# Loads moved at two places of an attention and feed-forward kernel: its first rows of x, and o at the seam before the last stage

## The reference

```
h   = layernorm(x)
q, k, v = h@Wq.T + bq + ocr_bias, h@Wk.T + bk, h@Wv.T + bv
s   = q k / sqrt(32) + 0.1 where |i - j| <= 2          (per head)
x   = x + softmax(s) v @ Wo.T + bo
h2  = quantise(layernorm(x))      # blocks of 32, FP6 grid, scale from the block's largest |value|
x   = x + h2 @ quantise(W).T + bias
```

## Time and profile before

| | us |
|---|---|
| median of three runs | 4157.7 |
| the profiled execution | 4158.59 |
| its span, first to last instruction | 4156.7 |
| granted TensorE clock, mean | 0.990 |
| TensorE (PE) busy | 4040.4 (97%) |
| VectorE (DVE) busy | 3359.5 (81%) |
| GpSimd (POOL) busy | 3034.7 (73%) |
| ScalarE (ACT) busy | 2407.3 (58%) |

### The profile page before, as it was taken

One profiled execution on the slowest core, in us unless ns is written; L12 is line 12 of the kernel. 1 busy time (PEld: TensorE's weight loads), 2 busy tenths in 40 slices (PEclk: granted clock), 3 DMA queues, 4 the chain that ended last, 5 costly groups with the idle time before them and its releaser, 6 DMA issues.

```text
span 4156.7 us, 59570 instructions
## 1 busy us (share of the span) xinstructions
PE 4040.4 (97%) x21328; PEld 2538.1 (61%) x21328; DVE 3359.5 (81%) x5630; ACT 2407.3 (58%) x4651; POOL 3034.7 (73%) x1121
## 2 busy tenths in 40 slices
PE   8999999999999999999999999999999999988999
PEld 6788875555555555555555555555555555546877
DVE  6444568888888888888888888888888898867887
ACT  2222216667667666767676666766676766662322
POOL 2111107888988889899888888888888888874553
PEclk9999999999999999999999999999999999988999
DMA  7888759899999999999999999999999899986665
GB/s 244 266 265 256 230 158 178 182 213 189 200 197 198 197 193 206 189 212 185 206 186 208 189 200 199 193 201 190 203 189 207 182 210 183 213 190 176 176 170 110
DMA packets 292318, 825.16 MB, mean 199 GB/s; under 512 B 28880, under 2 KB 95440, under 8 KB 229584
## 3 DMA queue, kind: packets, MB, share of 16 engines
q0 software_dynamic: 73008, 486.57, 59.5%
q1 hardware_dynamic: 219040, 335.09, 28.7%
HBM read 211.82 MB, written 156.24 MB: 89 GB/s over the span
## 4 chain that ended last, share of the span: by engine, by line
PE 78%; DVE 14%; ACT 3%; DMA 3%; POOL 1%; issue 1%; SPq 1%; POOLq 0%; ACTq 0%; DVEq 0%
PE ps_a L871 20%; PE ps_a L857 20%; PE ps_b L836 17%; PE ps_p L481 12%; DVE part_max L1048 8%; PE ps_b L902 4%; PE ps_b L949 3%; DVE p_sb L1075 3%; ACT p_sb L1024 2%; PE ps_b L882 1%; DMA q_st<-shift 1%; POOL pair L1221 1%; PE ps_a L932 1%; DMA p_sb<-o_d 1%; DMA q_lo_d<-s_lo 0%
## 5 line engine op out<-in xcount | busy, mean ns | idle before, releaser
L1048 DVE TENSOR_REDUCE part_max<-ps_b 128x1 f32<-128x512 f32 x4016 | 2464.1, 678 | 379.9 <-PE ps_b L836 379.7
L1024 ACT ACTIVATE p_sb<-ps_a 128x512 f32<-128x512 f32 x4096 | 2083.6, 614 | 731.5 <-PE ps_a L857 727.4
L1221 POOL TENSOR_TENSOR pair<-p_sb 128x2048 f32<-128x2048 f32 x512 | 2452.5, 4810 | 73.4 <-ACT p_sb L1024 57.9
L871 PE MATMUL ps_a<-p_sb,v_sb 128*32 128x512 f32 x8192 | 996.8, 603 | 37.8 <-DVE p_sb L1075 23.6
L857 PE MATMUL ps_a<-q_st,k_odd 97*128 97x512 f32 x2048 | 844.3, 415 | 12.4 <-DMA q_st<-shift 9.4
L857 PE MATMUL ps_a<-q_st,k_even 97*128 97x512 f32 x2048 | 845.4, 413 | 6.7 <-PEq L163 3.8
L836 PE MATMUL ps_b<-k_odd,q_st 96*128 96x512 f32 x2048 | 813.1, 397 | 0.0
L836 PE MATMUL ps_b<-k_even,q_st 96*128 96x512 f32 x1968 | 783.3, 398 | 0.0
L857 PEld LDWEIGHTS ps_a<-q_st,k_odd 97*128 97x128 f32 x2048 | 387.9, 190 | 337.2 <-issue 213.4
L857 PEld LDWEIGHTS ps_a<-q_st,k_even 97*128 97x128 f32 x2048 | 388.3, 190 | 322.7 <-issue 219.3
L871 PEld LDWEIGHTS ps_a<-p_sb,v_sb 128*32 128x32 f32 x8192 | 224.0, 109 | 524.2 <-ACT p_sb L1024 318.9
(11 more groups left out here) (114 smaller groups left out, 2861.4 us busy)
## 6 DMA issues: line engine op xcount, KB each, us to landing
pair<-pair POOLq DMA_DIRECT2D x448, 1024.0 KB, 8.8
q_st<-q_hi_d SPq DMA_DIRECT2D x128, 256.0 KB, 7.1
xin<-in_x SPq DMA_DIRECT2D x16, 1024.0 KB, 8.6
xb_d<-xb SPq DMA_DIRECT2D x16, 1024.0 KB, 5.7
q_hi_d<-s_hi SPq DMA_DIRECT2D x64, 256.0 KB, 6.3
q_lo_d<-s_lo SPq DMA_DIRECT2D x64, 256.0 KB, 7.3
k_hi_d<-s_hi SPq DMA_DIRECT2D x64, 256.0 KB, 3.4
k_lo_d<-s_lo SPq DMA_DIRECT2D x64, 256.0 KB, 4.3
```

The source lines that it names most:

```text
L871: last = nc.tensor.matmul(ps_a[h * HD:(h + 1) * HD, RING_S, :], v_sb[:, kt, h * HD:(h + 1) * HD], p_sb[:, s % SLOTS, h, :], start=(kt == 0 ...
L1024: nc.scalar.activation(p_sb[:, s % SLOTS, h, :], ps_s[:, (HG * s + h) % RING_S, :], ACT.Exp, scale=SCALE).then_inc(p_ready, 1)
L1048: nc.vector.tensor_reduce(part_max[:, unit % 2, col, n:n + 1], ps_m[:, max_place(unit, j) % RING_M, :], AX.X, ALU.max).then_inc(max_taken, 1)
L1221: nc.gpsimd.tensor_tensor(pair[:, m % PAIR_RING], p_sb[:, s % SLOTS], p_sb[:, (s + 1) % SLOTS], ALU.add).then_inc(paired, 1)
```

## The change

At the start, the load of chunk 0's x becomes four loads of one tile each, each with its own semaphore, and `moments(0)` waits for them one by one; the common counter `x_loaded` counts from chunk 1 on. ScalarE takes a square root of a constant before the first real one. At the seam between attention and finish: `load_o(1)` stands after `put_shift` of the last unit instead of five steps ahead of it; the four loads of `load_rec(2)` stand at steps 11 to 14 of the last unit instead of after `load_xb(1)`; `load_o(2)` stands ahead of `load_xb(1)`. For that, odd chunks from 3 on use `p_sb[:, 3]` and even ones `o_first`, where it was the other way round. TensorE projects three tiles of chunk 1 instead of two ahead of `turn_x(0)`. ScalarE does `normalise(1)` ahead of `o_highs(2)` instead of after it.

```diff
+            for t in range(TT):
+                sp.dma_start(xin[:, t, :], x_ch[0][:, t, :]).then_inc(x_first[t], 16)
-            sp.dma_start(xin[:], x_ch[0]).then_inc(x_loaded, 16)
...
             def moments(c):
-                v.wait_ge(x_loaded, 16 * c + 16)
+                if not isinstance(c, int) or c > 0:
+                    v.wait_ge(x_loaded, 16 * c)
                 for t in range(TT):
+                    if isinstance(c, int) and c == 0:
+                        v.wait_ge(x_first[t], 16)
...
             act.wait_ge(consts, 6)
+            nc.scalar.activation(root[:], eps[:], ACT.Sqrt)
             std_of(0)
...
         def o_raw(c):
-            return p_sb[:, 3] if c > 1 and c % 2 == 0 else o_first
+            return p_sb[:, 3] if c > 1 and c % 2 == 1 else o_first
...
-                    at_least(sp, o_split, NHG * (c - 1))
+                    at_least(sp, o_split, NHG * (2 if c == 2 else c - 1))
...
-                    if unit == NU - 2 and kt == 10:
+                    if unit == NU - 2 and kt == KT - 1:
                         load_o(1)
+                    if unit == NU - 1 and 11 <= kt < 11 + NHG:
+                        load_rec(2, (kt - 11,))
...
+            load_o(2)
             load_xb(1)
-            load_rec(2)
             sp.wait_ge(pv_done, ST)
             sp.wait_ge(paired, NM)
-            load_o(2)
             load_xb(2)
...
-                    out_project(c + 1, (0, 1))
+                    out_project(c + 1, (0, 1, 2) if c == 0 else (0, 1))
...
-                    out_project(c + 1, (2, 3))
+                    out_project(c + 1, (3,) if c == 0 else (2, 3))
...
                 high(c)
+                if c == 0:
+                    normalise(1)
                 if c + 2 < NCH:
                     o_highs(c + 2)
-                if c + 1 < NCH:
+                if 1 < c + 1 < NCH:
                     normalise(c + 1)
```

More of the change, by code:

```diff
@@ L136, in project @@
     w_loaded = [sem(f"w_loaded{i}") for i in range(3)]
+    x_first = [sem(f"x_first{i}") for i in range(TT)]
     consts, bias_ready = sem("consts"), sem("bias_ready")
@@ L173, in project @@
         std, rstd, eps = sb("std", [P, TT]), sb("rstd", [P, TT]), sb("eps", [P, 1])
+        root = sb("root", [P, 1])
         x_hi, x_lo = sb("x_hi", [P, KB, CH], F32R), sb("x_lo", [P, KB, CH], F32R)
@@ L202, in add_bias @@
             def add_bias(c):
-                pool.wait_ge(x_loaded, 16 * c + 16)
+                at_least(pool, x_loaded, 16 * c)
                 at_least(pool, xb_out, 16 * c)
```

## The result

The change makes the kernel slower: 4161.17 us median (4146.72 to 4172.83, 20 runs) against 4152.58 (4142.87 to 4166.67, 20 runs), ratio 1.002 (1.0011 to 1.0029), 4.6 to 12 us. 4143.5 was forecast, with 4159 as the range's upper end. The forecast starts from the three-run median of 4157.7, and the 20 runs of before have theirs 5.1 us lower: as a change it was -14.2, and +8.6 is measured. The profiled execution took 4161.27 with a span of 4159.4 and a mean granted clock of 0.991; the one of before 4158.59, 4156.7 and 0.990.

A forecast was written before the change was run, and what follows sets the result against it. It took TensorE as the bound (78% of the span, VectorE 14%), with holes. Start -2.0, shift and rec(2) together +0.5, order -12.8: -14.3 on 4158.6 gives 4144.3; median 0.9 below, 4143.5, range 4128 to 4159.

The forecast's parts named there:

- `rec(2)` ahead of `xb(0)`: Seam: xb(0) lands behind rec(2) at 3740 to 3741, turn_x(0) stays at 3758; +0.5 us, bounds -10 and +15.
- ScalarE's order and the third tile: Between turn_x(0) and turn_x(1): wait for last_sum and slow stretch go, third tile fills a hole; -12.8 us, between 5 and 14.3.
- The `shift` DMA: Seam: with load_o(1) behind it, shift lands at about 3671; attention ends at about 3740, 3 us gained of 8.5.
- The start: Chunk 0's normalisation: w_lo starts 2.2 us earlier and xb ends at 17.9; gain 2.0 us, between 0.6 and 2.2.
- C: Seam rival, chance 0.20: the queue costs more, xb(0) at 3745, xb(1) late by 5 or GpSimd's low parts on the chain; 4152.
- D: Seam rival, chance 0.05: slower, rec(1)'s packets move at 24 in 4 us, scale_o(1) starts at some 3738; 4166.
- the spread: Seam alternative: rec(2) spread evenly over sixteen engines holds xb(0) up by a quarter as much, and 3 us are kept.

The follow-up runs named there:

- experiment 1: Changed kernel with the four loads of rec(2) put back after load_xb(1): 4155.88 us, ratio 1.0007 to the kernel before.
- experiment 7: Changed kernel with only one chunk's rec loads spread over sixteen DMA engines, in two kernels: rec(2) alone 4140.65 us, ratio 0.999; rec(1) alone 4148.17 us, 1.0001.
- experiment 6: Changed kernel with the load of wd_lo moved behind load_xb(1): 4148.58 us, ratio 0.9987 to the kernel before.
- experiment 4: Kernel before with only normalise(1) ahead of o_highs(2) and three tiles of out_project(1) ahead of turn_x(0): 4149.94 us, ratio 0.9998.
- experiment 5: Kernel before with only the rec loads spread over all sixteen DMA engines: 4126.43 us, ratio 0.9935.
- experiment 3: Kernel before with only the changed start (four tile loads of x, root of a constant): 4157.23 us, ratio 1.0013.
- experiment 9: Kernel before with only the changed start, the root tile placed last so that no address moves: 4144.37 us, ratio 0.9991.
- experiment 2: Changed kernel with all rec loads spread over sixteen DMA engines: 4126.81 us, ratio 0.994 to the kernel before.
- experiment 10: Changed kernel with the rec loads spread over sixteen engines and the root tile last in the projection's memory: 4127.97 us, ratio 0.9939 to the kernel before.
- experiment 11: Kernel before with spread rec loads, changed start (root tile last), normalise(1) first and three tiles; loads at their old places: 4116.59 us, ratio 0.9929.
- experiment 8: Kernel before with an unused tile added in front of x_hi, moving the addresses behind it by 32 bytes: 4157.16 us, ratio 1.0001.

## Why the prediction was wrong

**The step that failed** is "`rec(2)` ahead of `xb(0)`", priced at +0.5 with bounds of -10 and +15 on the start of `turn_x(0)`. Measured: 21.3 us more between the last `shift` and `turn_x(0)` (89.8 to 111.1), and 20 by experiment 1, outside the bounds. The mechanism named there is right (`xb(0)` behind `rec(2)` on four engines); the size is wrong: `xb(0)` was to land 12 to 13 us after its issue and took 27.1. The step let `rec(2)` begin when it is issued. But the queue on those four engines still held `rec(1)`'s tail and the shares of `wd_hi` and `wd_lo` behind it until 3727. The weights stand in SP's timeline of before, between `rec(1)` and `xb(0)`, and the working never counted them. Experiment 7 prices `rec(2)` being narrow at 15 of the 20; experiment 6 has 13 for `wd_lo`, with a quiet stretch in it (the two overlap).

**ScalarE's order and the third tile**, -12.8. In the changed kernel the stretch from `turn_x(0)` to `turn_x(1)` shrank by 15.6, as worked out. But its gain was counted as if it were the step's own. It hung on the one that failed: without the early `rec(2)` the order alone gives 5 in the profile and nothing in the time (experiment 4), because o(2)'s low parts are late next. The prediction named them as next and found them in time, with `rec(2)` early. And with wide `rec` loads the stretch is 28.0 us without this step (experiment 5): the wait for the bank that it removes hung on the narrow loads as well. At `turn_x(1)` the whole seam is 5.6 us later (129.1 to 134.7), where these two steps had -12.3.

**The `shift` DMA.** The end is nearly right, by luck. `shift` lands in 3.9 us. But o(1) was to land 22 us after its issue and took 7.7, and `rec(1)` was to be through 22 us behind it and `scale_o(1)` starts 43.6 us behind it: `rec(1)` was priced at half of what it took. Counted from the last `shift`, `scale_o(1)` starts at 51.9 us where 44.3 was forecast (3712 less 3667.7), but takes 2.50 us and not 9.09, so the attention ends at 73.4 (72.3 forecast, 75.5 before). Three errors nearly cancel. The 2 us that the profile shows as gained aren't shown to be the move's, since experiment 3 has the same exchange of one wait for another without it; the residual then waited for `xb(0)` anyway.

**The start**, -2.0. In chunk 1 it is -1.2. The three more issues, taken at 0, cost 0.9 us at `w_lo`: wq lands at 9.9 and the bias at 11.8 instead of 8.85 and 10.99. In this profile nothing of it is left at the first `shift`, issued at 725.72 us and before at 725.43. Experiment 3 has the whole slower by 1 to 10 us, experiment 9 has it faster by 0 to 7; they differ by 32 bytes of address, which no step had.

**The sum** in times: start with moved addresses +5.4 (experiment 3), order -0.8 (4), `rec(2)`'s place +5.3 (4161.17 less 4155.88), together +9.9 for a measured +8.6. Each is uncertain by 4 to 5 us, so the sum only agrees; and the places of o(1) and o(2) were never taken back alone. The rivals: C had the mechanism (one queue, `xb(0)` late) but `xb(0)` at 3745, 11 us too early. D had the sign, by `rec(1)` at 24 packets in 4 us: it had `scale_o(1)` start at 3738, and it started at 3717. The prediction's own test (wrong if `turn_x(0)` moves by more than 5) came true.

The Trainium skill's rule ("DMA: Bandwidth & Descriptors", "Why a DMA increments its semaphore by 16 and not by 1"), that a DMA splits its slowest dimension over the engines, was weighed for `rec(2)` against `xb(0)` alone. The prediction gave the spread 3 us there; experiment 7 gives 15.0 for `rec(2)`. The trace agrees with the rule: `rec(2)` by itself keeps 25.7% of the engines busy.

## What to carry to other kernels

A DMA that uses four of the sixteen engines delayed the full-width DMAs behind it in its queue for as long as its own tail lasted (1 MB in 27.1 us, and in 15.5 with the narrow load made wide): before moving a load ahead of another, list all that is queued between them and give each its share on the narrow engines. Make the narrow load wide (split its slowest dimension, here one head with all groups) before moving it. And when the gain of one step needs an operand that another step brings, price the two as one.

## What had not been expected of the hardware

**The later chunks.** From `turn_x(1)` to `turn_x(15)` it is 329.7 us in experiments 2, 5 and 10, and 332.4 in experiment 11, against 336.6 to 341.8 with narrow loads there in before, after, experiments 1, 3, 4 and 8 and experiment 7's `rec(2)` alone. It is 334.1 in experiment 9 and 333.9 with `rec(1)` alone spread, and 329.7 in experiment 6 whose loads of these chunks are all narrow. So the width of the loads isn't the only cause; what else sets it stays open.

**32 bytes.** ScalarE's evictions of the last projection chunks, each behind one more group of products (start, duration; the idle before is the wait for TensorE): in the kernel before they are 3.46 us apart,

```profile
588.93 0.69 ACT L433 ACTIVATE s_hi<-ps_p,bias 128x512 fp32r<-128x512 f32 x1 [2.77 <-PE ps_p L481]
592.39 0.69 ACT L433 ACTIVATE s_hi<-ps_p,bias 128x512 fp32r<-128x512 f32 x1 [2.77 <-PE ps_p L481]
```

and in experiment 8, which only shifts addresses, 3.49 to 3.50:

```profile
588.60 0.69 ACT L434 ACTIVATE s_hi<-ps_p,bias 128x512 fp32r<-128x512 f32 x1 [2.81 <-PE ps_p L482]
592.09 0.69 ACT L434 ACTIVATE s_hi<-ps_p,bias 128x512 fp32r<-128x512 f32 x1 [2.81 <-PE ps_p L482]
```

TensorE is granted its full clock (1.00, 2.4 GHz) in 585 to 600 us in both, and is busy for all of the 15 us. 3.45 to 3.47 against 3.49 to 3.50 parts all six profiles with unmoved addresses from all eight with moved ones. From the restart in chunk 1 to the last eviction of the projection the six took 544.7 to 550.1 us, the eight 549.1 to 554.5. On the mean that is 547 against 552, but they overlap, and experiment 8's time allows anything from 5 us lost to 5 gained. That the products' pace depends on the address is shown; which operand does it, and what it costs the kernel, is not.
